# A state-space scan inside a twelve-stage decoder on one Trainium2 core: the scan stage rewritten as 64 unrolled steps, with the convolution folded into the projection and the products with B taken from TensorE

## Chip, cores and metric

One Trainium2 chip, one core. The time is the device time of one execution in microseconds; the kernel before was run three times (median 1649.15, 1648.54 to 1650.21). Everything but the final store lives in the core's on-chip memory. The program is one long sequence of twelve layers ("stages"), each followed by a layer normalisation; the change concerns the fourth of them and the hand-over to it.

## What is computed

The input is x of 4 batches x 256 tokens x 128 features. Stage L1a is a Mamba layer, the reference reads (cut):

```
xn = layer_norm(x) * g + b
u, z = split(xn @ W_in.T)                          # 256 channels each
u = silu(sum_k conv_w[:, k] * pad(u)[k : k+256] + conv_b)   # 4 taps, causal
dt_in, B, C = split(u @ W_x.T)                     # 8, 16 and 16 columns
dt = softplus(dt_in @ W_dt.T + dt_bias)
A = -exp(A_log)
h[t] = exp(dt[t] * A) * h[t-1] + dt[t] * B[t] * u[t]   # for each channel and n < 16
y[t] = sum_n h[t] * C[t]
y = (y + u * D) * silu(z)
out = x + y @ W_out.T
```

After it the decoder adds x once more and normalises the sum, which is the input of the next stage, L1x.

## The kernel before

A feature lies on one of 128 partitions, time runs along the free dimension. The 256 channels make two halves of 128, so a tile for one batch is 128 x 512 (two halves of 256 time steps). All matmuls but those named are float32.

**Class Mamba (L1767 to L2146).** `vector` clears `dA` and `up` (L2013, L2014), takes the statistics of all eight 128-token tiles of X (L2018 to L2024) and writes the eight normalised tiles XN (L2026). TensorE transposes them (L1846), ScalarE copies them out with gain and bias into XNT (L1939). Per batch, `inputs` projects XNT to u and z (L1854, four matmuls of 256 columns), ScalarE copies u out (L1944), VectorE runs the convolution as eight instructions of 256 columns (`convolve`, L2035 and L2037), ScalarE takes silu of both (L1949, L1951). `dt_inputs` and `dts` are the matmuls that give dt_in (L1862), B and C (L1867) and dt's argument (L1873); `arguments` adds the bias (L2045), `logs` on ScalarE computes the parts of softplus (L1959 to L1962), `steps_of_time` on VectorE finishes dt and dt*u (L2065 to L2070) and makes u*D (L2072). `parts` (L2052 to L2059) splits B and C into three bfloat16 parts so that a bfloat16 matmul with a one-hot stationary operand can spread one row of B or C over all partitions (`spread_b` L1890, `spread_c` L1896).

For each batch there are 16 steps, one for each n. A step consists of: `spread_b` on TensorE, its copy to on-chip memory on ScalarE (`b_copy`, L1971), two Exp instructions for dA on ScalarE (`decays`, L1979), the product dB = dt*u*B on GpSimd (L2146, 128x512), the scan along time on VectorE (L2081, with dA and dB both in SBUF), the product with C on VectorE (L2090), and the sum over n on TensorE with the identity (L1884, 512 columns). dA, dB and hC have three buffers, h has two. Three batches run in a hardware loop whose body also prepares the next batch: the convolution is placed between the steps n = 2 to 9, `inputs` at n = 0, silu at n = 11. But `parts`, `steps_of_time` and the last part of `logs` stand behind the last step of a batch, as do the addition of u*D and the gate (L2105, L2106), the output matmuls (L1916) and the two additions that give Z (L2114, L2115).

**Class LayerEnd (L143 to L236)** is the normalisation after each stage: statistics of Z (L177, L180), Ln and Exp on ScalarE for the reciprocal root (L196, L197), three small refinement steps (L138 to L140), eight tiles of X (L188), their transposes (L203) and two copies to XT (L217 or L223, and L227). With `early=True` the first six tiles are handled inside the stage, and only the last two behind it. `keep_warm` (L83) issues bfloat16 matmuls on zeros to a spare bank. The end of L0f, the stage before Mamba, is an early one; that of Mamba is not, and handles all eight tiles after the last batch.

Each engine works through its own instructions in order; the order of the steps is written out by hand, and engines wait for each other through counting semaphores. What an engine must wait for holds up everything behind it in its own order.

## Time and profile before

| | us |
|---|---|
| median of three runs | 1649.15 |
| the profiled execution's own time | 1648.05 |
| its span on the core | 1646.3 |
| last X tile of the end of L0f to the first scan | 528.1 to 561.15 |
| first scan to the start of the 64th | 561.15 to 769.38 |
| start of the 64th scan to the end of the last copy to XT | 769.38 to 784.06 |

Over the whole span TensorE is busy 82%, VectorE 62%, ScalarE 43%, GpSimd 24%. Times in timelines count from the start of the span. A row of a timeline gives start, duration, engine, line, operation, what is written and read, the count of instructions merged in it, and in brackets the idle time before it. One float32 matmul appears as two MATMUL instructions (and two weight loads, PEld); a transpose or a bfloat16 matmul as one. The durations of successive matmuls overlap, so the cost of one in a dense row is the distance of the starts. PEclk is the granted TensorE clock as a share of full speed, 1.00 being 2.4 GHz and 0.50 being 1.2 GHz.

### The profile page before, as it was taken

The page shows a single profiled execution, that of the slowest core. Times are in us where ns is not written, and L with a number is a line of the kernel's source. Part 1 is how long each engine was busy: PE and PEld are TensorE (multiplying, and loading weights), DVE is VectorE, ACT ScalarE, POOL GpSimd, SP SyncE. Part 2 cuts the span into 40 slices and gives each one's busy share as a digit, 9 for nine tenths or more (in the row PEclk, how much of TensorE's full clock was granted, in tenths as well). Part 3 has the DMA queues.
Part 4 walks back from the last instruction along what each step waited for, and adds up shares of the span by engine and source line. Part 5 has one row for each costly group of instructions (what it writes and reads, how often), then busy time and mean ns, then how long its engine had stood idle before and what let it go on. Part 6 is the DMA issues. An engine that isn't in the chain of part 4 may idle for free.

```text
span 1646.3 us, 24843 instructions
## 1 busy us (share of the span) xinstructions
PE 1350.1 (82%) x9010; PEld 839.1 (51%) x9062; DVE 1024.8 (62%) x2330; ACT 700.9 (43%) x1979; POOL 398.6 (24%) x313
## 2 busy tenths in 40 slices
PE   7999766887876567656897647999998999989997
PEld 4665643555554222212554434555566666656664
DVE  2556567666655688888667776755576455643334
ACT  4555324565653545453464303632234555422222
POOL 1333005444420325437400025200100333310000
PEclk9999988999998665678998969999999999999999
DMA  8000000000002200000000000000000000000000
GB/s 355 1 1 1 1 1 1 1 1 2 1 1 89 118 1 0 0 0 0 1 2 0 1 1 1 2 1 1 0 2 2 1 1 1 1 1 0 1 0 13
DMA packets 4217, 24.99 MB, mean 15 GB/s; under 512 B 1168, under 2 KB 3216, under 8 KB 3472
## 3 DMA queue, kind: packets, MB, share of 16 engines
q1 hardware_dynamic: 4112, 23.59, 3.6%
q8 instruction: 66, 1.08, 0.3%
q14 instruction: 39, 0.32, 0.1%
HBM read 23.06 MB, written 0.52 MB: 14 GB/s over the span
## 4 chain that ended last, share of the span: by engine, by line
PE 63%; DVE 20%; issue 8%; ACT 6%; POOL 1%; DMA 1%; DVEq 0%; SPq 0%; POOLq 0%; ACTq 0%
PE PS L1067 5%; PE PS L637 5%; PE PS L1052 4%; PE PS L1053 4%; PE PS L321 4%; PE PS L353 3%; PE PS L333 3%; PE PS L703 3%; DVE arena L2090 2%; PE PS L294 2%; PE PS L302 2%; PE PS L362 2%; PE PS L296 2%; PE PS L315 2%; PE PS L2270 1%
## 5 line engine op out<-in xcount | busy, mean ns | idle before, releaser
L545 POOL TENSOR_TENSOR arena<-arena,small 128x768 f32<-128x768 f32 (+1 forms) x64 | 107.7, 1683 | 225.7 <-DVE small L488 116.7
L873 DVE TENSOR_REDUCE arena<-PS 128x2 f32<-128x512 f32 (+1 forms) x192 | 108.8, 609 | 53.5 <-PE PS L631 52.5
L800 ACT ACTIVATE arena<-PS 128x512 f32<-128x512 f32 (+1 forms) x192 | 92.2, 532 | 107.2 <-PE PS L637 107.2
L1156 DVE TENSOR_TENSOR arena<-arena,PS 128x512 f32<-128x512 f32 x82 | 56.4, 688 | 116.0 <-ACT arena L1089 116.0
L2146 POOL TENSOR_TENSOR arena<-arena 128x512 f32<-128x512 f32 x64 | 103.9, 1643 | 89.5 <-DVE arena L2081 33.0
L1089 ACT ACTIVATE arena<-PS 128x512 f32<-128x512 f32 x82 | 49.0, 597 | 166.0 <-PE PS L1053 166.0
L425 ACT ACTIVATE arena<-PS,small 128x256 f32<-128x256 f32 (+1 forms) x256 | 110.8, 453 | 0.0
L637 PE MATMUL PS<-arena 32*128 32x256 f32 (+1 forms) x768 | 97.5, 370 | 14.0 <-DVE arena L873 8.8
L2081 DVE TENSOR_TENSOR_SCAN arena<-arena 128x512 f32<-128x512 f32 x64 | 94.0, 1473 | 21.7 <-ACT arena L1979 14.3
L1884 PE MATMUL PS<-arena,w_consts 128*128 128x512 f32 x128 | 95.1, 841 | 3.3 <-DVE arena L2090 3.3
L631 PE MATMUL PS<-arena 32*128 32x256 f32 (+1 forms) x768 | 94.5, 371 | 2.2 <-DVE arena L873 1.6
L496 DVE COPY arena<-PS 128x768 f32<-128x768 f32 (+1 forms) x64 | 69.5, 1086 | 34.6 <-PE PS L333 34.5
L637 PEld LDWEIGHTS PS<-arena 32*128 32x128 f32 x768 | 63.8, 185 | 42.8 <-ACT arena L800 31.0
L1067 PEld LDWEIGHTS PS<-w_last,arena 128*128 128x128 f32 x512 | 67.0, 191 | 31.1 <-issue 28.9
L2771 POOL TENSOR_TENSOR arena<-arena 128x512 f32<-128x512 f32 x32 | 40.5, 1267 | 156.2 <-DVE arena L2605 156.2
L1067 PE MATMUL PS<-w_last,arena 128*128 128x128 f32 x512 | 67.7, 275 | 1.0 <-DVE arena L1156 1.0
L1052 PE MATMUL PS<-XT,w_last 128*128 x128 | 66.9, 605 | 0.0
L1053 PE MATMUL PS<-XT,w_last 128*128 x128 | 66.2, 599 | 0.0
L321 PE MATMUL PS<-arena 64*128 64x256 f32 (+1 forms) x512 | 65.9, 376 | 0.0
L2486 ACT ACTIVATE arena<-PS,small 128x128 f32<-128x128 f32 x128 | 45.3, 366 | 46.7 <-DVE small L2633 46.6
L333 PE MATMUL PS<-w_consts,arena 128*128 128x128 f32 x448 | 60.2, 274 | 4.7 <-POOL arena L545 4.6
L631 PEld LDWEIGHTS PS<-arena 32*128 32x128 f32 x768 | 59.6, 185 | 7.1 <-DVE arena L873 4.3
(408 smaller groups left out, 3121.9 us busy)
## 6 DMA issues: line engine op xcount, KB each, us to landing
w_last<-in_last SPq DMA_DIRECT2D x1, 8260.0 KB, 22.6
w_rest<-in_rest SPq DMA_DIRECT2D x1, 5898.5 KB, 36.8
w_last<-in_first SPq DMA_DIRECT2D x1, 4532.5 KB, 21.1
w_last<-in_first SPq DMA_DIRECT2D x1, 2176.0 KB, 10.1
X<-in_x SPq DMA_DIRECT2D x1, 512.0 KB, 4.5
CT<-in_ctxT SPq DMA_DIRECT2D x1, 512.0 KB, 10.8
out<-X SPq DMA_DIRECT2D x1, 512.0 KB, 3.2
w_consts<-in_consts SPq DMA_DIRECT2D x1, 373.0 KB, 3.2
```

The lines of the kernel that those rows point to most:

```text
L321: ins = pe.matmul(PS[:, bank + r, col:col + n], self.QT[rows, p, t * P:(t + 1) * P], self.KT[rows, p, 0:n], start=False, stop=True, skip_g ...
L333: ins = pe.transpose(PS[:, 4 + r, b:b + P], self.Pr[:, i % 3, r, a:a + P], c.ident)
L425: ins = a.activation(self.Pr[:, i % 3, r, col:col + n], PS[:, i % 2 * 2 + r, col:col + n], ACT.Exp, bias=self.nm[:, i % 3, r, t:t + 1], sc ...
L545: g.tensor_tensor(p, p, ri, ALU.mult).then_inc(self.pn_done.sem, 1)
L631: return pe.matmul(PS[:, bank, t * n:(t + 1) * n], self.QP[rows, i % 8, t * P:(t + 1) * P], self.KP[rows, i % 8, t * step:t * step + n], s ...
L637: return pe.matmul(PS[:, 3 + q % 3, t * n:(t + 1) * n], self.KP[rows, i % 8, t * P:(t + 1) * P], self.QP[rows, i % 8, t * step:t * step + ...
L873: v.tensor_reduce(dst, src, AX.X, ALU.max, negate=True).then_inc(self.mx_done.sem, 1)
L1052: pe.matmul(PS[:, j % 2, :], w[:, 0:P], x, start=True, stop=True)
L1053: pe.matmul(PS[:, 2 + j % 2, :], w[:, P:2 * P], x, start=True, stop=True)\
L1067: ins = pe.matmul(PS[:, 4 + e % 2, t * P:(t + 1) * P], self.Hd[0:rows, j % 3, t * P:(t + 1) * P], w, start=(f == 0 and t == 0), stop=(f == ...
L1884: pe.matmul(acc, c.ident, self.hC[:, n % 3, :], start=(n == 0), stop=(n == self.N - 1))\
L2146: g.tensor_tensor(two(self.dB[:, n % 3, :]), self.dtu, b, ALU.mult).then_inc(self.db_ready.sem, 1)
```

## The change

The four batches become one straight sequence of 64 steps g = 16 b + n, without a loop, on every engine.

- The convolution is gone as vector work. A GpSimd instruction of 128 x 1024 multiplies, once, the four taps into copies of the u half of W_in (`WK`); u is then the sum of four matmuls per half over shifted windows of XNT, which has three zero columns ahead of each batch. The convolution's bias goes into the silu instruction.
- B comes with time on partitions (four small matmuls with u stationary, 16 columns). GpSimd builds diagonal matrices from it (`diagonals`, two instructions of 128 x 512 for four steps), dt*u is transposed once per batch (`turn`), and dB is made on TensorE as four matmuls of 128 columns (`drive`) into a bank of PSUM, from which the scan reads it. `b_copy` and the GpSimd product are gone. C is spread with a float32 matmul of 16 rows and 256 columns; `parts` is gone.
- u*D is added on TensorE with diagonal matrices (two matmuls of 256 columns per batch). One vector instruction gives y, one gives Z.
- The bias of dt goes into the two ScalarE passes Abs and Relu; the rest of softplus is five instructions of 128 x 512 on GpSimd (`chain`), for the first batch on VectorE.
- All preparations of batch b+1 are placed among the steps of batch b: on TensorE `inputs` at n = 0, 1, 2, `selections` at 6, `steps` at 8, `turn` at 13; on ScalarE silu at 6, copies at 8, `logs` at 10, the copy of the turned product at n = 1 of the next batch; on VectorE `gate` and `finish` of the batch before at 3 and 5. dA has four buffers.
- The end of Mamba is an early one: six tiles are normalised inside the last batch. The end of L0f makes no XT, since Mamba does not read it, and issues 20 warming matmuls instead. Mamba's own statistics go in groups of two and six tiles.

The diff, cut to its core:

```diff
@@ LayerEnd @@
     def tensor(self, pe):
-        if not self.last:
+        if self.turned:
             keep_warm(self.c, pe, self.spare, 5 if len(self.groups) == 2 else 14)
             self.transposes(pe, len(self.groups) - 1)
             keep_warm(self.c, pe, 3, 4)
+        elif not self.last:
+            keep_warm(self.c, pe, self.spare, 20)
@@ Mamba, tensor @@
+        def inputs(b, part):
...
+            if part < 2:
+                for k in range(4):
+                    ins = pe.matmul(PS[:, self.bank(b, part), part * 256:part * 256 + 256], self.WK[:, k, part * P:(part + 1) * P],
+                                    self.XNT[:, b, k:k + 256], start=(k == 0), stop=(k == 3), skip_group_check=True)
+            else:
...
+                for j in range(2):
+                    ins = pe.matmul(PS[:, 1, j * 256:j * 256 + 256], self.win[:, (2 + j) * P:(3 + j) * P],
+                                    self.XNT[:, b, 3:259], start=True, stop=True, skip_group_check=True)
+            ins.then_inc(self.uz_done.sem, 1)
+        def selections(b):
+            pe.wait_ge(self.us_ready.sem, self.us_ready.at(0, b + 1))
+            u = self.u[:, b % 2, :]
+            for j in range(2):
+                pe.matmul(PS[0:48, 0, 0:256], self.wdc[:, j, :], u[:, j * 256:j * 256 + 256],
+                                start=(j == 0), stop=(j == 1), skip_group_check=True)
+            for t in range(2):
+                for j in range(2):
+                    ins = pe.matmul(PS[:, 0, 256 + t * 16:272 + t * 16], u[:, j * 256 + t * P:j * 256 + t * P + P],
+                                    self.wB[:, j, :], start=(j == 0), stop=(j == 1), skip_group_check=True)
+            ins.then_inc(self.dc_done.sem, 1)
+        def turn(b):
+            pe.wait_ge(self.chain_step.sem, self.chain_step.at(0, 5 * b + 5))
+            pe.wait_ge(self.bt_ev.sem, self.bt_ev.at(0, b + 1))
...
+        def drive(g):
+            b, n = divmod(g, self.N)
+            if n == 0:
+                pe.wait_ge(self.tr_ev.sem, self.tr_ev.at(0, b + 1))
+            if n % 4 == 0:
+                pe.wait_ge(self.diag_ready.sem, self.diag_ready.at(0, g // 4 + 1))
...
+                pe.wait_ge(self.sc_ready.sem, self.sc_ready.at(0, g - 1))
+            for t in range(2):
+                for j in range(2):
+                    ins = pe.matmul(PS[:, 2 + g % 2, j * 256 + t * P:j * 256 + t * P + P],
+                                    self.dtuT[:, b % 2, t, j * P:(j + 1) * P], self.diag[:, g % 12 * 2 + t, :],
+                                    start=True, stop=True, skip_group_check=True)
+            ins.then_inc(self.db_done.sem, 1)
+        def spread(g):
...
+            if g >= 2:
+                pe.wait_ge(self.hc_ready.sem, self.hc_ready.at(0, g - 1))
+            pe.matmul(PS[:, 4 + g % 2, 0:256], self.onehot[32:48, n:n + 1].to_broadcast([16, P]),
+                      self.CB[32:48, b % 2, :], start=True, stop=True).then_inc(self.c_done.sem, 1)
+        def add(g):
...
+            pe.wait_ge(self.hc_ready.sem, self.hc_ready.at(0, g + 1))
+            pe.matmul(PS[:, bank, :], c.ident, self.hC[:, g % 3, :], start=(n == 0), stop=(n == self.N - 1),
+                      skip_group_check=True).then_inc(self.acc_done.sem, 1)
...
+        selections(0)
+        keep_warm(c, pe, 5, 2)
+        steps(0)
+        keep_warm(c, pe, 5, 36)
+        turn(0)
+        drive(0)
+        spread(0)
+        for i in range(self.G):
+            b, n = divmod(i, self.N)
+            if i + 1 < self.G:
+                drive(i + 1)
+                spread(i + 1)
+            if i >= 2:
+                add(i - 2)
+            if b and n == 4:
+                outputs(b - 1)
+            if b + 1 < B:
+                if n < 3:
+                    inputs(b + 1, n)
+                if n == 6:
+                    selections(b + 1)
+                if n == 8:
+                    steps(b + 1)
+                if n == 13:
+                    turn(b + 1)
@@ Mamba, scalar @@
+        def decays(g):
+            b, n = divmod(g, self.N)
+            if n == 0:
+                a.wait_ge(self.chain_step.sem, self.chain_step.at(0, 5 * b + 4))
+            if g >= 4:
+                a.wait_ge(self.sc_ready.sem, self.sc_ready.at(0, g - 3))
...
+                if n == 6:
+                    silus(b + 1)
+                if n == 8:
+                    selections(b + 1)
+                if n == 10:
+                    logs(b + 1)
+            elif n == 10:
+                self.end.root(a, 0)
@@ Mamba, vector @@
+        def scan(g):
+            v.wait_ge(self.da_ready.sem, self.da_ready.at(0, g + 1))
+            v.wait_ge(self.db_done.sem, self.db_done.at(0, g + 1))
+            if g >= 2:
+                v.wait_ge(self.hc_ready.sem, self.hc_ready.at(0, g - 1))
+            v.tensor_tensor_scan(self.h[:, g % 2, :], self.dA[:, g % 4, :], PS[:, 2 + g % 2, :], 0.0,
+                                 ALU.mult, ALU.add).then_inc(self.sc_ready.sem, 1)
...
+        for g in range(self.G):
+            b, n = divmod(g, self.N)
+            scan(g)
+            if g:
+                outputs(g - 1)
+            if b and n == 3:
+                gate(b - 1)
+            if b and n == 5:
+                finish(b - 1)
+            if b == B - 1 and n == 8:
+                self.end.early_stats(v)
+            if b == B - 1 and n == 13:
+                self.end.tiles(v, 0)
@@ Mamba, gpsimd @@
+        g.tensor_tensor(self.WK, self.WK, self.win[:, 0:256].unsqueeze(1).to_broadcast([P, 4, 256]), ALU.mult)\
+            .then_inc(self.wk_ready.sem, 1)
...
+        for b in range(B):
+            for q in range(4):
+                diagonals(4 * b + q)
+            if b + 1 < B:
+                self.chain(g, b + 1)
@@ build @@
-            s.end = LayerEnd(c, s.z_ready, last=i == len(names) - 1, early=isinstance(s, (Attention, NarrowAttention, LocalLayers)),
+            s.end = LayerEnd(c, s.z_ready, last=i == len(names) - 1, early=isinstance(s, (Attention, NarrowAttention, LocalLayers, Mamba)),
```

In `chain` the five instructions are: (ex + 1) - 1, ex - r, + relu, + ln, times u; each waits for the one before. `logs` is two Abs and two Relu of 256 columns, Exp and Ln of 512.

## Rows read from the trace of the kernel before

**Rows 1.** Windows: busy time of each engine, granted clock, DMA, in three stretches of the stage

```profile
core 0: us, PE busy (x) PEld busy (x) DVE busy (x) ACT busy (x) POOL busy (x), PEclk, DMA share, GB/s
528.00:561.15 33.15, 15.17 (x44) 8.51 (x45) 17.55 (x54) 14.41 (x24) 2.64 (x3) 0.65 0.56 239
561.15:769.38 208.23, 135.62 (x326) 48.84 (x325) 180.45 (x206) 103.58 (x228) 105.39 (x66) 0.69 0.00 0
769.38:784.06 14.68, 9.75 (x39) 4.56 (x41) 11.03 (x39) 1.11 (x3) 4.75 (x3) 0.99 0.00 1
```

**Rows 2.** Timeline, steps of the last batch: start, us, engine, line, form

```profile
758.64 1.44 DVE L2081 TENSOR_TENSOR_SCAN arena<-arena 128x512 f32<-128x512 f32 x1
758.96 8.63 POOL L2146 TENSOR_TENSOR arena<-arena 128x512 f32<-128x512 f32 x4
...
760.00 0.66 DVE L2090 TENSOR_TENSOR arena<-arena,PS 128x512 f32<-128x512 f32 x1
...
760.79 1.44 DVE L2081 TENSOR_TENSOR_SCAN arena<-arena 128x512 f32<-128x512 f32 x1
...
769.38 1.23 DVE L2081 TENSOR_TENSOR_SCAN arena<-arena 128x512 f32<-128x512 f32 x1
...
770.52 1.26 DVE L2090 TENSOR_TENSOR arena<-arena,PS 128x512 f32<-128x512 f32 x2
```

**Rows 3.** Timeline, one step of the first batch

```profile
577.61 1.20 DVE L2037 SCALAR_TENSOR_TENSOR arena<-arena,w_rest 128x256 f32<-128x256 f32 x1
...
577.93 1.91 PE L1884 MATMUL PS<-arena,w_consts 128*128 128x512 f32 x2
578.73 1.21 DVE L2081 TENSOR_TENSOR_SCAN arena<-arena 128x512 f32<-128x512 f32 x1
...
579.87 0.66 DVE L2090 TENSOR_TENSOR arena<-arena,PS 128x512 f32<-128x512 f32 x1
```

**Rows 4.** Groups by line and shape, 528 to 561 us

```profile
L2037 DVE SCALAR_TENSOR_TENSOR arena<-arena,w_rest 128x256 f32<-128x256 f32 x6 | 2.9, 485 | 0.2
...
L2026 DVE TENSOR_SCALAR arena<-X,mv,rs 128x128 f32<-128x128 f32 x8 | 2.1, 342 | 0.0
...
L2018 DVE BATCH_NORM_STATS2 bn<-X 128x6 f32<-128x128 f32 x8 | 1.6, 278 | 0.0
...
L2013 DVE MEMSET arena<- 128x1536 f32 x1 | 1.3, 1338 | 0.3 <-issue 0.3
L1949 ACT ACT_TABLE_LOAD x1 | 1.3, 1283 | 0.0
...
L1962 ACT ACTIVATE arena<-arena 128x512 f32<-128x512 f32 x1 | 0.6, 629 | 0.0
```

**Rows 5.** Groups by line and shape, 561 to 777 us: busy, mean ns, idle before

```profile
L2146 POOL TENSOR_TENSOR arena<-arena 128x512 f32<-128x512 f32 x63 | 102.6, 1649 | 76.2 <-DVE arena L2081 33.0 <-ACT arena L1971 23.5 <-DVE arena L2072 19.6
...
L2081 DVE TENSOR_TENSOR_SCAN arena<-arena 128x512 f32<-128x512 f32 x64 | 94.0, 1473 | 21.7 <-ACT arena L1979 14.3 <-DVE arena L2037 2.6 <-DVE arena L2035 1.3
L1979 ACT ACTIVATE arena<-arena 128x255 f32<-128x255 f32 x127 | 56.8, 498 | 4.7 <-DVE arena L2081 4.3
```

**Rows 6.** Windows: a short stretch of the scan stage, and the dense one

```profile
596.00:600.00 4.00, 4.00 (x15) 1.64 (x14) 1.92 (x3) 2.31 (x7) 1.60 (x2) 1.00 0.03 6
1559.00:1570.00 11.00, 11.00 (x51) 6.91 (x50) 4.33 (x9) 2.39 (x4) 0.00 (x0) 1.00 0.00 0
```

**Rows 7.** Timeline, TensorE alone, dense stretches of later stages

```profile
1346.40 1.04 PE L333 MATMUL PS<-w_consts,arena 128*128 128x128 f32 x8
...
1560.63 1.05 PE L1067 MATMUL PS<-w_last,arena 128*128 128x128 f32 x8
1561.53 1.02 PE L1052 MATMUL PS<-XT,w_last 128*128 x2
1562.39 1.02 PE L1053 MATMUL PS<-XT,w_last 128*128 x2
```

**Rows 8.** Timeline, GpSimd, the last instruction before the scan stage's first product

```profile
545.21 1.04 POOL L2138 TENSOR_TENSOR arena<-arena,w_consts 128x512 f32<-128x512 f32 x1 [35.52 <-ACT arena L1951]
```

More of the change, by code:

```diff
@@ L200, in transposes @@
         c = self.c
-        for n in range(*self.groups[g]) if not self.last else ():
+        for n in range(*self.groups[g]) if self.turned else ():
             pe.wait_ge(self.x_tile.sem, self.x_tile.at(0, n + 1))
@@ L214, in vector @@
         self.tiles(v, g)
-        if not self.last and g == 0:
+        if self.turned and g == 0:
             v.wait_ge(self.xt_ps.sem, self.xt_ps.at(0, 1))
@@ L220, in scalar @@
         c, g = self.c, len(self.groups) - 1
-        if g == 1 and not self.last:
+        if g == 1 and self.turned:
             a.wait_ge(self.xt_ps.sem, self.xt_ps.at(0, 1))
@@ new lines, in scalar @@
+        normal(0, 2, 0, 1)
+        silus(0)
+        normal(1, 3, 1, 2)
+        normal(2, 4, 3, 1)
+        selections(0)
+        logs(0)
+        for g in range(self.G):
+            b, n = divmod(g, self.N)
+            if g == 0:
+                decays(0)
+                turned(0)
+            else:
+                decays(g)
+            if n == 1 and b:
+                turned(b)
+            if b + 1 < B:
[7 more added lines that the diff above has]
+                self.end.root(a, 0)
```

543 lines of the change are left out of this document (226 added, 317 removed).

## The prediction

> **What bounds the kernel now.** I read the windows first, to see where the stage begins and ends, then the groups of lines in it, then the timeline of single steps. The scan stage takes 33.15 us to its first scan, 208.23 us from the first to the last scan and 14.68 us to the last copy of XT [rows 1]. In the middle stretch VectorE is busy 180.45 of 208.23 us, TensorE 135.62, ScalarE 103.58 and GpSimd 105.39, and the granted TensorE clock averages 0.69: VectorE is the bound, and TensorE does most of its work at 1.2 GHz, where one sum over n takes 1.91 us [rows 3]. A single step shows what VectorE does. In the last batch, where nothing is prepared, scan follows scan after 760.79 - 758.64 = 2.15 us: 1.36 to the product with C, 0.79 from there to the next scan [rows 2]. With GpSimd idle the first part is 770.52 - 769.38 = 1.14 us [rows 2]. In the first batch a convolution instruction of 1.20 us stands in such a step [rows 3]; the same form took 0.485 us before GpSimd's products began [rows 4]. GpSimd's product takes 1.65 us in the mean and 8.63 / 4 = 2.16 us in the last batch [rows 2, 5]. The two engines hold each other up. The rest of the 208 us is preparation behind each batch's last step.
>
> **The sum: one step.** The change moves 512 columns of products per step to TensorE. Its three parts are priced from a dense stretch at clock 1.00 [rows 6]: four float32 matmuls of 128 columns are 1561.53 - 1560.63 = 0.90 us apart, one of 512 columns 1562.39 - 1561.53 = 0.86 [rows 7]. So `drive` is 0.90, `spread` (256 columns) half of 0.86 = 0.43, `add` 0.86: 2.19 us of TensorE per step. VectorE has 1.14 + 0.79 = 1.93 if the scan runs as it does with GpSimd idle. TensorE becomes the bound. There is a loop through both engines too: `spread`(g+1) waits for the product g-1, and the scan g+1 waits for `drive`(g+1). From a scan's start to the second next it is 1.14 (scan) + 0.66 (product) + 0.43 + 0.86 + 0.90, plus 0.1 each for two hand-overs and 0.15 for the last matmul's end (1.05 - 0.90 [rows 7]) = 4.34, or 2.17 per step. With the scan at 1.36 it is 2.28. The scan now has one operand in SBUF and one in PSUM, a form of which the trace has no row: below it is bounded by 1.14, above by 1.36 with GpSimd running. I take 2.25 for a step: 63 x 2.25 = 141.8 us.
>
> The Trainium skill ("SBUF — State Buffer", Who interferes with whom) says that a VectorE instruction with at most one SBUF input and no two-port mode does not contend with GpSimd. The rows agree as far as they go (two SBUF inputs: 1.36 against 1.14), and by that rule the step would be 2.19 and the total 4 us lower.
>
> **What lies between the steps.** TensorE being the bound, each insertion counts in full. Per prepared batch: `inputs` 10 matmuls of 256 columns at 0.43 = 4.3; `selections` 2 x 0.43 and four tiny ones, which load 128 columns of weights each as `drive` does, 0.9, = 1.8; `steps` 0.86; `turn` four transposes, half of eight at 1.04 [rows 7], = 0.5. That is 7.5 us, three times: 22.4. u*D costs 0.86 four times, 3.4. The output matmuls cost 0.90 three times, 2.7. Together 28.5. The vector instructions `gate` and `finish` (0.66 and less) fit into VectorE's 0.25 us of slack per step, at a stall of a few tenths; the 2.25 holds it. Before, all this (and `parts`) cost at most what 208.23 - 63 x 2.15 = 73 us leaves.
>
> **The new wait.** ScalarE must load another function table for Silu, Exp and Ln, 1.28 us each [rows 4]. Silu at n = 6 is hidden, for the four dA buffers are full then. `logs` at n = 10 starts when `steps` is done, after TensorE's n = 8: four half passes (1.8), Exp 0.63, table 1.28, Ln 0.63, table 1.28, then the pair for dA, 2 x 0.498 [rows 4, 5] = 6.6 us. At that moment the scan 9 is some 2.1 us old, so the scan 11 would be due 3.1 us later. VectorE waits for `decays`(11) about 3.5 us, behind it the product 10, and `spread`(12) on TensorE. Three times: 10.5 us. `chain` on GpSimd begins 2.5 us after `steps` and needs five instructions of 1.04 us alone [rows 8] to 2.16 beside VectorE [rows 2], 6 to 11 us; `turn` at n = 13 comes about 14 us after `steps`, counting the wait, so it is hidden. If the wait of ScalarE were gone, `turn` would be late instead, by up to 3 us. The diagonals (two instructions for four steps, at most 4.3 us of 9) are hidden. The pair for dA (1.0 us of each step) is too. In the last batch the early end puts six statistics (6 x 0.278), a refinement and six tiles (6 x 0.342) on VectorE, 4.3 us of which the slack takes some: 3.5.
>
> Loop: 141.8 + 28.5 + 10.5 + 3.5 = 184.3 against 208.2: -24 us.
>
> **Before the first scan.** Off the path go a memset (1.34), eight convolution instructions (8 x 0.485 = 3.9), six of the eight normalised tiles ahead of the first projection (1.6) [rows 4], and one pass each on VectorE and ScalarE less four half passes for one, 0.6. On it come six more matmuls of 256 columns (2.6) and the turned product in place of GpSimd's (0.8). The granted clock was 0.65 there [rows 1]; with 20 and 36 warming matmuls I expect the high level for most of it, worth 3. Sum -7; at the low level 0, and all of it at its best -10. GpSimd's product of the taps runs in the 35.52 us in which it idled [rows 8] and costs nothing.
>
> **Behind the last scan.** Six of eight statistics and tiles (0.75 x (2.2 + 2.7), by [rows 4]'s means 278 and 342) are -3.7, of which about 1 was overlapped; six transposes -0.8 [rows 7]; two vector instructions less, of 0.66 and 0.4, -1.1. Sum -5.
>
> **Total:** -24 - 7 - 5 = -36. The profiled execution took 1648.05, so 1612; the median of the runs stands 1.1 higher: 1613 us.
>
> **Rivals.** *TensorE keeps the low level (slower).* The place is the loop. Its 63 x 2.19 + 28.5 = 166.5 us of TensorE work hold at clock 1.00; at a granted mean c they are 166.5 / c. At the old 0.69 that is 241, with some 7 us of the waits left 248: +40, less 9 at the ends, so 1680 us. The point from which it decides: 166.5 / c + 14 = 208.2 + 9, c = 0.82. For it speaks that TensorE stayed at 0.69 while busy 65% of the time [rows 1]; against it, that it is at 1.00 where it was busy throughout, even for 4 us inside this stage [rows 6], and that it now never waits long but for three stops of 3.5 us. 6%.
>
> The Trainium skill ("TensorE: Matmul & The Clock Gate", HAM oscillation) says that pauses between bursts of matmuls bring the half rate back. By it each of the three stops would be followed by some steps at 1.2 GHz, 5 us or so apiece by the rows' prices, and the total near 1628, inside the range.
>
> *The hand-overs cost more.* A step with waits on three semaphores on TensorE costs 2.45, as when each group's first matmul starts cold; 63 x 0.2 = 12.6, and `chain` at 2.16 per instruction makes `turn` late by 3 us three times: 1613 + 22 = 1635. For it speaks that GpSimd's products did take 2.16 beside the scan. 16%.
>
> *ScalarE's wait is absorbed.* If `logs` starts earlier or Abs, Relu and Exp need no new table, and the step is 2.19, 10.5 + 4 go: 1599. 14%.
>
> *The scan from PSUM is slow, or the change fails of its purpose.* A scan 0.35 us longer makes VectorE's 2.28 the bound, near 1617, within the forecast. That the work moved to TensorE just eats the gain, at a mean clock near 0.82, is 1649: 2%.
>
> The forecast has 62%. A measurement of this kernel can tell some 0.2%, 3.3 us, from no change. The range holds the absorbed wait and the dear hand-overs: 1595 to 1636. Faster 0.93, same 0.02, slower 0.05.
>
> **What would show it.** Right: granted clock above 0.9 between the first and last scan; TensorE busy above 90%; scans 2.2 to 2.3 us apart in plain steps; a wait of VectorE for ScalarE's Exp near each batch's step 11; scans of 1.2 us, whether GpSimd runs or not; first scan at 554, last at 738. Wrong: scans over 2.4 us apart in plain steps; TensorE waiting for GpSimd (`turn`, diagonals) for more than 2 us a batch; a clock of 0.7.

## The result, and the profile after

The changed kernel takes 1627.45 us (median of 4 runs, 1626.36 to 1628.41) against 1648.85 for the kernel before (1647.86 to 1650.21): ratio 0.9871, 95% interval 0.9858 to 0.9884. It is 21.4 us faster where 36 were forecast. The profiled execution took 1626.36, its span is 1624.5.

The windows of the three stretches of the stage, as in [rows 1] (columns as there: stretch, length, busy time and instructions of PE, PEld, DVE, ACT, POOL, then the granted clock, DMA share and GB/s):

```profile
528.00:553.96 25.96, 22.53 (x106) 13.36 (x105) 9.63 (x40) 15.57 (x29) 6.21 (x6) 0.93 0.71 306
553.96:754.18 200.22, 193.25 (x911) 127.72 (x911) 119.34 (x153) 85.52 (x174) 47.28 (x41) 0.98 0.00 1
754.18:766.58 12.40, 8.21 (x35) 4.30 (x35) 8.21 (x19) 2.98 (x5) 4.75 (x3) 1.00 0.00 0
```

The prologue went from 33.15 to 25.96 us, the loop from 208.2 to 200.2, the stretch behind the last scan from 14.7 to 12.4. TensorE is now busy 193.25 of 200.22 us at clock 0.98, and VectorE 119 instead of 180. These three differences make 17.5 us of the 21.8 between the spans. The other 4.3 us lie behind the stage, in code that is the same in both kernels: from the last copy of XT to the end it took 862.24 us before and 857.92 after, and in the kernels below 859 to 866. TensorE was busy 759.0 us of it before and 753.6 after, VectorE 501.2 and 501.9. The change did not aim at these 4.3 us and the forecast has no term for them. So lengths inside the stage are compared below as well as totals.

The groups of lines in the loop, by form (busy, mean ns | idle before, and what ended it), to be held against [rows 5]:

```profile
L2104 DVE TENSOR_TENSOR_SCAN arena<-arena,PS 128x512 f32<-128x512 f32 x64 | 78.1, 1220 | 81.3 <-PE PS L1890 70.3 <-ACT arena L2021 10.3
...
L1890 PEld LDWEIGHTS PS<-arena 128*128 128x128 f32 x504 | 66.8, 196 | 21.8 <-issue 21.3
...
L2157 POOL TENSOR_TENSOR arena<-w_consts,arena 128x512 f32<-128x512 f32 x26 | 26.4, 1042 | 57.5 <-PE PS L1890 57.5
...
L1912 PEld LDWEIGHTS PS<-arena,w_consts 128*128 128x128 f32 x120 | 18.0, 190 | 20.2 <-issue 20.2
```

The scan (L2104) waits 70.3 us for `drive` (L1890) and 10.3 us for ScalarE's exponentials (L2021). The scan with one operand in PSUM takes 1.22 us whether GpSimd runs or not, and GpSimd's remaining product (the diagonals, L2157) 1.04 where its old one took 1.65. And the weight loads of `drive` and of `add` (L1912) each stand idle some 21 us for "issue", which nothing recorded explains. That is the first sign of what went wrong in the forecast.

The timeline of plain steps, on VectorE, TensorE and TensorE's weight loads (start, us, engine, line, form, idle before):

```profile
571.98 1.22 DVE L2104 TENSOR_TENSOR_SCAN arena<-arena,PS 128x512 f32<-128x512 f32 x1 [0.77 <-PE PS L1890]
...
574.55 1.22 DVE L2104 TENSOR_TENSOR_SCAN arena<-arena,PS 128x512 f32<-128x512 f32 x1 [0.77 <-PE PS L1890]
...
570.83 1.05 PE L1890 MATMUL PS<-arena 128*128 128x128 f32 x8
571.81 0.69 PE L1903 MATMUL PS<-arena,w_consts 16*128 16x256 f32 x2
572.44 1.12 PE L1912 MATMUL PS<-arena,w_consts 128*128 128x512 f32 x2
573.40 1.05 PE L1890 MATMUL PS<-arena 128*128 128x128 f32 x8
...
571.81 0.29 PEld L1903 LDWEIGHTS PS<-arena,w_consts 16*128 16x128 f32 x2
572.43 0.30 PEld L1912 LDWEIGHTS PS<-arena,w_consts 128*128 128x128 f32 x2 [0.33 <-issue]
```

A plain step is 574.55 - 571.98 = 2.57 us. From start to start `drive` (L1890) takes 0.98, `spread` (L1903) 0.63, `add` (L1912) 0.96, where the forecast had 0.90, 0.43 and 0.86. TensorE waits for no other engine here. VectorE waits 0.77 us for `drive` in each step, so TensorE sets the pace. The last two rows show that the load of `spread` starts with its own matmul, at 571.81, and that of `add` at 572.43, with the matmul at 572.44: neither runs ahead under the matmul before it.

### The profile page after: what moved, and what is told of

Its sections match the earlier page's. It is cut to its first block, busy times and chain, and to the rows that moved or that the text cites. A ratio compares the mean times of both kernels' runs of the same rounds, so it can differ in the third digit from the quotient of the medians.

```text
span 1624.5 us, 25636 instructions
## 1 busy us (share of the span) xinstructions
PE 1413.6 (87%) x9708; PEld 918.2 (57%) x9708; DVE 953.5 (59%) x2240; ACT 685.6 (42%) x1932; POOL 348.1 (21%) x293
## 4 chain that ended last, share of the span: by engine, by line
PE 72%; DVE 15%; ACT 6%; issue 4%; POOL 1%; DMA 1%; DVEq 0%; SPq 0%; ACTq 0%; POOLq 0%
PE PS L1071 6%; PE PS L641 5%; PE PS L1056 4%; PE PS L1057 4%; PE PS L325 4%; PE PS L1912 4%; PE PS L357 3%; PE PS L1890 3%; PE PS L337 3%; PE PS L707 3%; PE PS L1903 2%; PE PS L298 2%; PE PS L306 2%; PE PS L366 2%; PE PS L319 2%
## 5 line engine op out<-in xcount | busy, mean ns | idle before, releaser
L2104 DVE TENSOR_TENSOR_SCAN arena<-arena,PS 128x512 f32<-128x512 f32 x64 | 78.1, 1220 | 81.3 <-PE PS L1890 70.3
L641 PE MATMUL PS<-arena 32*128 32x256 f32 (+1 forms) x768 | 97.7, 371 | 13.8 <-DVE arena L877 9.5
L641 PEld LDWEIGHTS PS<-arena 32*128 32x128 f32 x768 | 64.0, 185 | 42.3 <-ACT arena L804 30.4
L1071 PEld LDWEIGHTS PS<-w_last,arena 128*128 128x128 f32 x512 | 66.9, 191 | 32.7 <-issue 28.7
L1890 PEld LDWEIGHTS PS<-arena 128*128 128x128 f32 x512 | 67.7, 196 | 22.7 <-issue 21.3
L2792 POOL TENSOR_TENSOR arena<-arena 128x512 f32<-128x512 f32 x32 | 40.6, 1269 | 156.0 <-DVE arena L2626 156.0
L2021 ACT ACTIVATE arena<-arena,w_rest 128x255 f32<-128x255 f32 x128 | 55.5, 497 | 41.7 <-DVE arena L2104 40.7
L1912 PE MATMUL PS<-arena,w_consts 128*128 128x512 f32 x128 | 72.5, 652 | 0.0
L1890 PE MATMUL PS<-arena 128*128 128x128 f32 x512 | 69.8, 280 | 0.7 <-ACT arena L2011 0.7
## 6 DMA issues: line engine op xcount, KB each, us to landing
w_last<-in_first SPq DMA_DIRECT2D x1, 4532.5 KB, 21.4
w_last<-in_first SPq DMA_DIRECT2D x1, 2176.0 KB, 10.3
```

Of the source, the lines that this page charges most:

```text
L641: return pe.matmul(PS[:, 3 + q % 3, t * n:(t + 1) * n], self.KP[rows, i % 8, t * P:(t + 1) * P], self.QP[rows, i % 8, t * step:t * step + ...
L1071: ins = pe.matmul(PS[:, 4 + e % 2, t * P:(t + 1) * P], self.Hd[0:rows, j % 3, t * P:(t + 1) * P], w, start=(f == 0 and t == 0), stop=(f == ...
L1890: ins = pe.matmul(PS[:, 2 + g % 2, j * 256 + t * P:j * 256 + t * P + P], self.dtuT[:, b % 2, t, j * P:(j + 1) * P], self.diag[:, g % 12 * ...
L1912: pe.matmul(PS[:, bank, :], c.ident, self.hC[:, g % 3, :], start=(n == 0), stop=(n == self.N - 1), skip_group_check=True).then_inc(self.ac ...
```

## Experiments

Below, "loop" is the length from the first to the last scan and "tail" that from the last scan to the last copy of XT; the changed kernel, called after, has 200.2 and 12.4 us. Each ratio is to the kernel before as it ran beside the kernel in question (medians 1648.0 to 1650.1), so totals of two kernels that differ by 2 us or less are not told apart.

### 1. ScalarE's logarithms two steps later

The question: what does the stop of VectorE for ScalarE cost in the end, and is it VectorE's wait or `turn` that decides?

```diff
-                if n == 10:
+                if n == 12:
                     logs(b + 1)
```

> `logs` moved on ScalarE from n = 10 to n = 12, so the pairs for scans 11 and 12 are made before it. Theory S (the three stops at step 11 cost what the trace of the changed kernel shows net: 585.60 to 590.83 is 5.23 instead of 2.57, of which the next scan wins back 0.64, so 2.0 to 2.2 each): 6.0 to 6.6 us less, 1621. Rival (the stop is cover for GpSimd's chain, and turn is late instead): 0 to 3 us less, with TensorE waiting before the transposes of dt*u.

1624.12 us (1622.64 to 1625.58), ratio 0.9851 (0.9828 to 0.9873). The stops are gone, plain steps stay at 2.57, `turn` isn't late, and the loop is 190.6 us, 9.6 shorter, more than the 6.0 to 6.6 expected. The total shows only 3.3 of that, half of what was expected of it, since in this profile the code before the first scan took 4.3 us longer and that behind the stage 4.5 (862.5 us). In after's timeline of VectorE the three stops can be read one by one. The first and the second:

```profile
585.60 1.22 DVE L2104 TENSOR_TENSOR_SCAN arena<-arena,PS 128x512 f32<-128x512 f32 x1 [2.02 <-PE PS L1890]
...
590.83 1.22 DVE L2104 TENSOR_TENSOR_SCAN arena<-arena,PS 128x512 f32<-128x512 f32 x1 [3.43 <-ACT arena L2021]
...
595.42 1.22 DVE L2104 TENSOR_TENSOR_SCAN arena<-arena,PS 128x512 f32<-128x512 f32 x1 [0.86 <-PE PS L1890]
...
643.91 1.22 DVE L2104 TENSOR_TENSOR_SCAN arena<-arena,PS 128x512 f32<-128x512 f32 x1 [3.43 <-ACT arena L2021]
...
654.30 1.22 DVE L2104 TENSOR_TENSOR_SCAN arena<-arena,PS 128x512 f32<-128x512 f32 x1 [2.92 <-PE PS L1890]
```

VectorE waits 3.43 us, close to the 3.5 forecast. But TensorE worked ahead meanwhile, so after the first stop a short step of 1.93 us follows (the next scan starts at 592.76): 595.42 - 585.60 = 9.82 us for three steps that otherwise take 7.71, a net cost of 2.1. The third stop costs 2.1 as well. The second began at 638.68 and needed 15.62 us for four steps that take 10.28, a net 5.3, since TensorE ran at its lower level for a while (experiment 10). 2.1 + 5.3 + 2.1 = 9.5, within 0.1 of the 9.6 that this kernel saves. The expectation had priced all three stops as the first.

### 2. A wait that is already met, inside `drive`

Is the dear step a price of waits, which TensorE's first instruction after a wait pays?

```diff
             for t in range(2):
+                if t:
+                    pe.wait_ge(self.wk_ready.sem, self.wk_ready.at(0, 1))
                 for j in range(2):
```

> One more wait per step on TensorE, on a semaphore that was reached long before, between the second and the third matmul of drive. Theory W (each wait keeps the weight load behind it from running ahead, so that it stands in the open at about 0.10 us): steps 2.67 instead of 2.57 us apart, 6 us more in all, 1634. Theory L (the 0.38 us above the sum of the matmuls comes from the loop through VectorE, scan to product to spread): no change, 1627, because TensorE would have that slack.

1634.35 us in two runs, ratio 0.9916 (0.9887 to 0.9945). Plain steps remain at 2.57 (scans at 569.02, 571.59, 574.16, 576.73), so a met wait costs nothing that one step shows. The total is 6.9 higher, of which the loop has 1.6 (201.8 us) and the rest lies outside it. The total alone would have misled.

The loop's 1.6 us come from the granted clock. In after it fell behind the second of ScalarE's three stops alone; here it fell behind each:

```profile
593.00:603.00 10.00, 8.14 (x28) 5.09 (x29) 6.62 (x8) 4.97 (x12) 7.04 (x7) 0.83 0.00 0
647.00:657.00 10.00, 7.97 (x32) 5.08 (x30) 5.93 (x7) 5.66 (x14) 7.72 (x7) 0.83 0.00 1
702.00:712.00 10.00, 7.97 (x29) 4.99 (x29) 6.24 (x7) 5.35 (x13) 7.39 (x7) 0.83 0.00 0
```

From the scan ahead of a stop, the five steps take 15.86 us in kernel 1, which has no stop; 17.97, 21.20 and 17.96 in after; and 19.58, 19.57 and 19.58 here. So the three stops cost 11.1 us net here and 9.5 in after.

### 3. `add` ahead of `spread`

Is it `add`, after the small matmul, that is dear, or whatever stands beside it?

```diff
                 drive(i + 1)
-                spread(i + 1)
             if i >= 2:
                 add(i - 2)
+            if i + 1 < self.G:
+                spread(i + 1)
```

> On TensorE the sum over n now stands before spread instead of behind it (drive, add, spread); spread's wait for VectorE's product is then met 0.9 us earlier. Theory W: 2.57 us per step as before, within 0.05. Theory L: the loop loses 0.86 us over two steps, so the step falls to 2.2 to 2.3 and the total by 17 us or more.

1624.69 us in two runs, ratio 0.9857 (0.9829 to 0.9886); plain steps 2.57 again. So neither theory holds: W (the price of a wait) wanted 2.67 in experiment 2, L (the loop through VectorE) wanted 2.2 to 2.3 here. The timeline of TensorE's weight loads:

```profile
571.15 0.30 PEld L1912 LDWEIGHTS PS<-arena,w_consts 128*128 128x128 f32 x2
572.22 0.29 PEld L1903 LDWEIGHTS PS<-arena,w_consts 16*128 16x128 f32 x2 [0.76 <-issue]
572.84 0.97 PEld L1890 LDWEIGHTS PS<-arena 128*128 128x128 f32 x8 [0.33 <-DVE arena L2105]
```

Now `add`'s load runs ahead of its matmul (571.15, the matmul starts at 571.26), and those of `spread` and of `drive` behind it don't (572.22 and 572.84, with their matmuls). In either order it is the load of the 16-row matmul and the one that follows it. The loop still fell to 191.1. TensorE now waits only 1.17 us at each stop instead of 2.04, as `add` is done ahead of the wait. The first stop's steps were 5.23, 1.93, 1.93 and 2.44, a net 1.25 instead of 2.1, and the clock did not fall after any stop. That accounts for 2.6 and 3.2 of the 9.1 us. Of the rest, 2.4 are the step behind `steps` (3.01 for 3.83, three times) and 0.6 that behind `selections` (4.46 for 4.65).

### 4. `add` in pairs

Two sums one behind the other share their hand-over. This takes a fourth hC buffer and its waits (cut here).

```diff
-            if i >= 2:
+            if i >= 3 and i % 2:
+                add(i - 3)
                 add(i - 2)
```

> The sums over n of two steps are issued together every second step, with one wait for both, and hC has four buffers; columns and matmuls stay. Theory W: one wait and one exposed weight load fewer in two steps, 0.05 us per step, 3 us less, 1624. Theory L: no change or worse, since the products of two steps are awaited together.

1640.34 us (1639.6 to 1643.62), ratio 0.9954 (0.9938 to 0.997), the loop 203.5, 3.3 longer; of the total's 12.9 us, 8.1 lie behind the stage. A miss: the steps alternate between 1.93 and 3.5 us (scans at 571.55, 573.48, 577.00), and in the short one TensorE waits for the product again ("[0.23 <-DVE arena L2114]"). That two buffers of dB and of C are too few for work in bunches is the likely reason; no run here varies them.

### 5. `spread` over all 128 rows

If it is the 16-row operand, the same broadcast with a one-hot column of 128 rows must remove the cost. CB is zeroed once, so that its unused rows add nothing to the sum.

```diff
-            pe.matmul(PS[:, 4 + g % 2, 0:256], self.onehot[32:48, n:n + 1].to_broadcast([16, P]),
-                      self.CB[32:48, b % 2, :], start=True, stop=True).then_inc(self.c_done.sem, 1)
+            pe.matmul(PS[:, 4 + g % 2, 0:256], c.ident[:, 32 + n:33 + n].to_broadcast([P, P]),
+                      self.CB[:, b % 2, :], start=True, stop=True).then_inc(self.c_done.sem, 1)
...
+        v.memset(self.CB, 0.0).then_inc(self.cb_clear.sem, 1)
```

> `spread` takes a one-hot column of the identity as a stationary operand of 128 rows (instead of 16 rows at partition 32) and all 128 rows of CB, of which the unused ones are zero; columns and waits stay. Theory R (the 0.38 us per step above the sum of the matmuls stands before and behind the 16-row matmul, because weight loads do not run ahead across it): the weight loads of spread and of add start before the matmul ahead of them has ended, the steps fall from 2.57 to 2.19 to 2.3 us, the loop by 15 to 22 us and the total to 1606 to 1613. Theory I (the cost is one of issuing the instructions of TensorE, or of its waits): nothing changes, 2.57 us and 1627.

1610.26 us (1609.2 to 1611.55), ratio 0.976 (0.9744 to 0.9776): 17 us faster than after by one edited matmul and the memset that it needs. The loop is 181.4, 18.9 shorter. Its timeline of steps:

```profile
570.13 1.22 DVE L2107 TENSOR_TENSOR_SCAN arena<-arena,PS 128x512 f32<-128x512 f32 x1 [0.41 <-PE PS L1891]
...
572.31 1.22 DVE L2107 TENSOR_TENSOR_SCAN arena<-arena,PS 128x512 f32<-128x512 f32 x1 [0.38 <-PE PS L1891]
...
568.98 1.05 PE L1891 MATMUL PS<-arena 128*128 128x128 f32 x8
569.87 0.60 PE L1904 MATMUL PS<-arena,w_consts 128*128 128x256 f32 x2
570.31 1.02 PE L1913 MATMUL PS<-arena,w_consts 128*128 128x512 f32 x2
571.17 1.05 PE L1891 MATMUL PS<-arena 128*128 128x128 f32 x8
...
569.77 0.30 PEld L1904 LDWEIGHTS PS<-arena,w_consts 128*128 128x128 f32 x2
570.09 0.41 PEld L1913 LDWEIGHTS PS<-arena,w_consts 128*128 128x128 f32 x2
```

A step is 2.18 us, and `drive`, `spread`, `add` are 0.89, 0.44 and 0.86 apart, the forecast's terms to a hundredth. The loads start 0.10 and 0.22 us before their matmuls.

The Trainium skill ("TensorE: Matmul & The Clock Gate", Step-by-step: what each phase is for) says that the queue pulls a weight load ahead of a running matmul when their row groups don't conflict or the load goes to the background buffer, and that the number of rows of the weights doesn't matter for its time. The trace agrees on the load's own time: 0.29 us for `spread` with 16 rows and 0.30 with 128. What the rows change is when it starts: with 16 it isn't pulled ahead, nor is the next, and the step takes 2.57 us instead of 2.18.

The trace of the kernel before held this already, in other stages. A load of 128 rows behind a 128-row matmul (L611 behind L615), then one behind 32-row matmuls (L631):

```profile
785.82 0.76 PEld L611 LDWEIGHTS PS<-CT,w_rest 128*128 128x128 f32 x2
786.25 1.02 PE L611 MATMUL PS<-CT,w_rest 128*128 128x256 f32 x2
...
787.68 1.15 PE L631 MATMUL PS<-arena 32*128 32x256 f32 x16
788.75 0.30 PEld L611 LDWEIGHTS PS<-CT,w_rest 128*128 128x128 f32 x2 [0.33 <-issue]
788.76 1.12 PE L611 MATMUL PS<-CT,w_rest 128*128 128x512 f32 x2
```

The first runs 0.43 us ahead, the second 0.01. It is so throughout that trace: of the float32 loads of 128 rows and columns for a matmul that follows another without a gap, none of the 56 behind 32-row weights and none of the 63 behind 64-row weights runs ahead, and none of the 58 behind weights of 128 rows but 64 columns; but all 59 behind the 96-row bfloat16 weights of the old `spread_b` and `spread_c` do, by 0.11 us or more. Where neighbours of 32 rows follow each other, loads do run ahead, by up to 0.39 us. So the rows fit a cost of the change between a short and a full operand, not of shortness alone.

### 6 and 7. The full-height `spread` with the later logarithms, and with the order of 3 as well

> The full-row spread together with logs at n = 12. If both act for themselves: the loop 9 to 10 us below that of the full-row spread alone, total 1597 to 1604. Rival (with faster steps GpSimd's chain of 7.2 us is late, and TensorE waits before the transposes of dt*u): less than half of the 9 us is kept.

> As the run before, and the sum over n ahead of spread. With the stops gone the order should bring little: 0 to 3 us less. If it brings over 3 us, the order helps in plain steps too, by giving VectorE's product more time.

The first: 1601.26 us (1599.64 to 1602.27), ratio 0.9703 (0.9687 to 0.972), loop 168.9. The second: 1597.8 (1597.34 to 1598.17), ratio 0.9683 (0.9667 to 0.9699), loop 167.3. Taken one after the other, the loop fell by 18.9 us for the rows, 12.4 for the stops and 1.6 for the order. With the shorter step the stops were dearer than in experiment 1 (9.6): against kernel 6 they cost experiment 5 a net 4.7, 3.0 and 4.7, and the clock fell after the first and the third, to 0.85 and 0.90 in stretches of 10 us. In kernel 7 TensorE was busy 166.5 of 167.3 us at clock 1.00, so little but its own work is left in this loop.

### 8. A scan with both operands in SBUF

The scan reads dA for both operands; the products dB are still made but not used. This tells whether the steady 1.22 us comes from the operand in PSUM or from GpSimd's lighter load.

```diff
-            v.tensor_tensor_scan(self.h[:, g % 2, :], self.dA[:, g % 4, :], PS[:, 2 + g % 2, :], 0.0,
+            v.tensor_tensor_scan(self.h[:, g % 2, :], self.dA[:, g % 4, :], self.dA[:, g % 4, :], 0.0,
```

> The scan takes dA as both operands, so it reads two tensors from on-chip memory and none from PSUM; dB is still made but not read (the result leaves dB out). Theory P (two operands in SBUF make the scan and GpSimd hold each other up): scans of 1.4 us and more where GpSimd runs, GpSimd's instructions of 1.04 us stretched to 1.3 to 2.2, first-to-last scan 0 to 5 us longer because TensorE has the bound. Rival (the 1.22 us is due to something else): scans of 1.22 us throughout.

1633.15 us in one run, loop 204.4. Its timeline, a stretch where GpSimd works:

```profile
595.49 1.04 POOL L2157 TENSOR_TENSOR arena<-w_consts,arena 128x512 f32<-128x512 f32 x1
...
595.68 1.93 DVE L2104 TENSOR_TENSOR_SCAN arena<-arena 128x512 f32<-128x512 f32 x1 [0.64 <-PE PS L1890]
...
598.32 1.23 DVE L2104 TENSOR_TENSOR_SCAN arena<-arena 128x512 f32<-128x512 f32 x1
...
598.41 1.97 POOL L2157 TENSOR_TENSOR arena<-w_consts,arena 128x512 f32<-128x512 f32 x1
```

Both scans stand beside a product of GpSimd, and of each two the one that starts first keeps its length. The product of 595.49 took its usual 1.04 us, and the scan that began 0.19 behind it 1.93. The scan of 598.32 took 1.23, and the product that began 0.09 behind it 1.97. The products' mean rises from 1.04 to 1.46 us, the longest scan is 2.11. With one operand in PSUM (after) no scan takes over 1.22 us and the products' mean stays at 1.04. The Trainium skill's rule ("SBUF — State Buffer", Who interferes with whom), of which [rows 2] showed only the half with two inputs, holds here in both halves.

### 9. The next stage's memset in four parts

After's tail is 2.7 us longer than forecast. Its timeline shows two normalised tiles at 2.70 us beside a memset of the next stage:

```profile
762.81 2.70 DVE L190 TENSOR_SCALAR X<-Z,mv,rs 128x128 f32<-128x128 f32 x2
...
761.86 3.51 POOL L971 MEMSET arena<- 128x4096 f32 x1
```

The pair ends at 765.51 and the memset at 765.37. The same memset stood in the kernel before:

```profile
777.85 3.51 POOL L967 MEMSET arena<- 128x4096 f32 x1
...
780.38 2.66 DVE L188 TENSOR_SCALAR X<-Z,mv,rs 128x128 f32<-128x128 f32 x8
```

There the tiles began 0.98 us before it ended; the early end brings the last two to where 2.56 us of it are left. On top of kernel 7:

```diff
-        g.memset(self.V, 0.0).then_inc(self.cleared.sem, 1)
+        for n in range(0, 8, 2):
+            ins = g.memset(self.V[:, n:n + 2, :], 0.0)
+        ins.then_inc(self.cleared.sem, 1)
```

> The fastest kernel so far (spread over 128 rows, logarithms at step 12, add ahead of the spread) with the next stage's memset of V on GpSimd issued in four parts of 128x1024. Theory M (the memset of 3.51 us held the last two X tiles: 2.70 us for the pair in after, where the tiles before took 0.60 for two): the stretch from the last scan to the last XT copy falls from 12.4 us by 1 to 2, the two last tiles take 0.6 to 1.3 us together, and the kernel is 1595.8 to 1596.8, 1 to 2 us below the same without the split. Rival (the tiles wait for something else, or the four parts hold them just as long, one after the other): the stretch keeps its length within 0.3 us and the kernel stays at 1597.3 to 1598.2.

1597.35 us (1596.86 to 1598.56), ratio 0.9693 (0.9677 to 0.9709). The same two groups, in this kernel:

```profile
729.83 1.04 DVE L190 TENSOR_SCALAR X<-Z,mv,rs 128x128 f32<-128x128 f32 x2
...
728.88 3.77 POOL L972 MEMSET arena<- 128x1024 f32 x4
```

The pair takes 1.04 us and the tail 10.32 instead of 12.01: 1.7 gained there, as expected. The medians differ by 0.45 us, within their own spread: the gain is shown in the stage, not in the total. In the two profiles the code behind the stage took 3.0 us longer here (863.6 against 860.6) and that ahead of the first scan 1.8 less.

### 10. No warming matmuls

The 20 + 4 + 2 + 2 + 36 matmuls that only keep TensorE busy ahead of the first scan are left out of after.

```diff
-            keep_warm(self.c, pe, self.spare, 20)
+            pass
...
-            keep_warm(c, pe, 5, warm)
...
-        keep_warm(c, pe, 5, 2)
         steps(0)
-        keep_warm(c, pe, 5, 36)
```

> After without the matmuls that only keep TensorE busy ahead of the first scan. If they earn their place (the clock of the prologue, 0.93 in after, falls to 0.5 to 0.8 and its matmuls double), the stretch from the stage's first instruction to the first scan grows from 26.0 us to 29 to 32 and the total by 3 to 6 us, to 1630 to 1634; the loop keeps its 200.2 within 1.5, its clock at 0.95 or more from the second batch on. If the clock is held by the projections anyway, the stretch stays within 1 us of 26.0 and the total within 1.5 us of 1627.5.

1648.69 us (8 runs, 1646.89 to 1653.22), ratio 1.0009 (0.9999 to 1.002): the whole gain of the change is gone. Both cases expected were wrong. From the last X tile to the first scan it takes 28.2 us (clock 0.62) instead of 25.9, only 2.3 more, but the loop grew by 17.2, to 217.4. Of these, 4.3 are its first two steps, before any stop, and 12.9 lie at the three stops. The windows behind the stops:

```profile
600.00:610.00 10.00, 9.36 (x23) 5.78 (x24) 4.18 (x6) 3.75 (x9) 5.96 (x6) 0.53 0.01 2
660.00:670.00 10.00, 10.00 (x26) 5.94 (x26) 3.90 (x5) 1.76 (x4) 4.01 (x5) 0.55 0.01 2
...
720.00:730.00 10.00, 10.00 (x27) 6.08 (x27) 3.60 (x4) 0.91 (x2) 1.93 (x2) 0.50 0.01 2
```

After each of ScalarE's three stops TensorE ran 10 to 14 us at 1.2 GHz. After has the same stops, with the same wait of TensorE, and its clock fell after the second alone. Its windows there:

```profile
640.00:650.00 10.00, 7.96 (x34) 5.39 (x33) 4.49 (x6) 7.93 (x15) 9.49 (x8) 0.86 0.00 1
650.00:660.00 10.00, 10.00 (x41) 6.36 (x40) 5.10 (x7) 3.20 (x7) 3.26 (x4) 0.80 0.00 0
```

And the timeline of TensorE at a stop, first after, then the kernel of this experiment, in a fence each:

```profile
645.76 0.69 PE L1903 MATMUL PS<-arena,w_consts 16*128 16x256 f32 x2 [2.04 <-DVE arena L2112]
...
647.58 1.92 PE L1890 MATMUL PS<-arena 128*128 128x128 f32 x8
```

```profile
600.64 1.22 PE L1902 MATMUL PS<-arena,w_consts 16*128 16x256 f32 x2 [2.04 <-DVE arena L2109]
...
603.65 1.92 PE L1889 MATMUL PS<-arena 128*128 128x128 f32 x8
```

The wait is 2.04 us in both. In after the matmul behind it still runs at the full rate (0.69) and `drive` at half (1.92 for 1.05); here already the first is slow (1.22). Without the warming, the first stop and its half rate cost 610.52 - 593.55 = 16.97 us for four steps of 2.57, a net 6.7 against 2.1 where the clock held.

The warming alone doesn't decide whether the clock falls. Of the kernels that keep it, with the same wait of 2.03 to 2.04 us at each stop, it fell after one stop in after and in experiment 11, after two in experiment 12, and after all three in experiments 2 and 4, in 10 of 15 cases. Experiment 2 changes nothing ahead of the first scan. In experiment 3, where TensorE waits 1.17 us, it fell after none. Nor does the warming bound how low it goes: in experiment 8 it was 0.50 from 647 to 657 us. Shown is that without the warming the gain is lost, in all 8 runs; whether the missing matmuls themselves did it, or the later and slower start of the loop that came with it, is open, since no run has one without the other. By the five steps of experiment 2, a stop cost 2.1 us net where the clock held and 3.7 to 8.6 where it fell (22.81, 22.80 and 24.43 us here). In kernels 1, 6, 7 and 9 there is none, and the clock is 1.00 throughout.

### 11. The stage's end late, as before

```diff
-            s.end = LayerEnd(c, s.z_ready, last=i == len(names) - 1, early=isinstance(s, (Attention, NarrowAttention, LocalLayers, Mamba)),
+            s.end = LayerEnd(c, s.z_ready, last=i == len(names) - 1, early=isinstance(s, (Attention, NarrowAttention, LocalLayers)),
```

The calls that went with it (statistics at n = 8, tiles at n = 13, the first transposes) are taken out too.

> After with the stage's end as it was in before: statistics, X tiles and their transposes all behind the last scan. The early end costs the loop nothing where VectorE has slack, so if it is worth what its hidden work is (two sets of tiles and transposes of four channel groups each, 2.14 us a set in before, less the copies that TensorE's loop makes wait), the stretch from the last scan to the last XT copy grows from 12.4 to 14 to 15.5 us and the total by 1.5 to 3 us, to 1629 to 1630.5, the loop staying within 1 us of 200.2. If the insertions cost TensorE's loop as much as they save, the loop falls by 1 to 2 us and the total stays within 1 us of 1627.5.

The two runs lie at 1630.5 and 1639.2 us (ratio 0.9919, 0.9888 to 0.995), too far apart to compare with after by the total. In the profile of the first the tail is 13.8 instead of 12.4 and the loop 199.3 instead of 200.2. That is just below the 14 to 15.5 expected, with the loop as expected. So in after the early end earns 1.4 us behind the last scan and costs 0.9 in the loop, a net 0.5. With the memset out of its way (experiment 9) its tail is 1.7 shorter still.

### 12. `spread` over 48 rows

Which matters, that the operand starts at row 32 or that it is short? The edit is shown against kernel 5:

```diff
-            pe.matmul(PS[:, 4 + g % 2, 0:256], c.ident[:, 32 + n:33 + n].to_broadcast([P, P]),
-                      self.CB[:, b % 2, :], start=True, stop=True).then_inc(self.c_done.sem, 1)
+            pe.matmul(PS[:, 4 + g % 2, 0:256], c.ident[0:48, 32 + n:33 + n].to_broadcast([48, P]),
+                      self.CB[0:48, b % 2, :], start=True, stop=True).then_inc(self.c_done.sem, 1)
```

> Spread with a one-hot of 48 rows from row 0 (after: 16 rows from row 32, plain step 2.57; the 128-row form: 2.18 to 2.21). If only a full-height operand keeps the weight loads hidden, a plain step is 2.55 to 2.60 and the kernel 1623 to 1628. If what hurts is that the operand starts at row 32 and not that it is short, a plain step is 2.18 to 2.25, and the kernel 1608 to 1613.

1631.27 us in two runs, ratio 0.9898 (0.9878 to 0.9917); loop 200.3, as in after. The weight loads:

```profile
571.49 0.29 PEld L1904 LDWEIGHTS PS<-arena,w_consts 48*128 48x128 f32 x2
572.12 0.30 PEld L1913 LDWEIGHTS PS<-arena,w_consts 128*128 128x128 f32 x2 [0.33 <-issue]
```

Their durations and the idle time between them are after's, and the step is 2.57, as the first case expected of the step. It is the height, not the start row: 16 and 48 rows cost 0.39 us a step more than 128. No run has a float32 `spread` of a height between 48 and 128. The total is 3.8 above after's, outside the 1623 to 1628 expected, with the same loop and tail, which again is the code outside the stage (862.7 us behind it, against 857.9).

## Why the prediction was right or wrong

**Right in its main mechanism, short by one term, and helped by luck.** The time fell in the range, and TensorE became the bound at a high clock: 0.98 in the loop against "above 0.9", busy 97% against "above 90%", a scan of 1.22 us against 1.2, the first scan at 553.96 against 554, GpSimd never waited for by TensorE. The slower rival, TensorE at the low level throughout, is refuted by the clock of 0.98. Two of the signs named for being right did not come: scans 2.2 to 2.3 us apart and the last one at 738 (it started at 754.18). One of those named for being wrong did: scans over 2.4 us apart in plain steps. Inside the stage 36 us were forecast and 17.5 came, less than half; the other 4.3 us between the spans are code that the change doesn't touch, and no credit to the forecast.

**The step that failed is "I take 2.25 for a step".** It measured 2.57, so 63 x 0.32 = 20.2 us were missing. The sum of three prices from dense rows [rows 7] was right in itself: with a full-height `spread` the step is 2.18. But [rows 7] shows 128-row matmuls following one another, and `spread` was priced as half of one, by its columns alone. It has 16 rows, and the load of a short operand and the one after it don't run ahead of the matmul before. The rows of L611 in experiment 5 show that the trace of before had this to read. The rival "hand-overs cost more" had 2.45, a size near the truth with the wrong cause: a further met wait costs a step nothing (experiment 2), the order neither (3), the rows all of it (5, 12).

**The loop's account.** Forecast 184.3, measured 200.2. The steps give +20.2. The three stops cost 9.5 instead of 10.5: VectorE's wait was 3.43 as forecast (3.5), but two of them cost 2.1 net, since TensorE had worked ahead, and one 5.3. Insertions and the last batch's early end were put at 22.4 + 3.4 + 2.7 + 3.5 = 32.0; without stops the loop is 190.6, of which 63 x 2.57 = 161.9 are steps and 28.7 are left, so -3.3. Most of that is the early end, put at 3.5 and worth 0.9 by experiment 11. Together +20.2 - 1.0 - 3.3 = +15.9.

**The clock.** The forecast's sentence on pauses, that each stop would be followed by steps at 1.2 GHz with the total near 1628, met the total by chance: in after one stop of three was, and most of the missing time lies in the plain steps. In experiments 2 and 4 all three are, and without the warming matmuls too. The Trainium skill's rule ("TensorE: Matmul & The Clock Gate", HAM oscillation) is borne out as a possibility of each pause, not as its certain result. The 3 us that the forecast gave the warming for the prologue were 2.3; that leaving it out would lengthen the loop by 17.2 us was not foreseen at all.

**Before the first scan** -7 was forecast and -7.2 measured, though the parts were not measured apart from the warming.

**Behind the last scan** -5 was forecast and -2.3 measured. Of the missing 2.7, 1.7 are the next stage's memset, which held two tiles (experiment 9). [rows 4] priced those tiles at 342 ns with nothing beside them; here 2.70 us for two. Another 0.4 is rounding, since the forecast's own terms, -3.7 + 1 - 0.8 - 1.1, make -4.6 and not -5. The last 0.6 was not taken apart.

**`turn` late** was part of the rival with 1635. It was not late in any kernel here: GpSimd's chain took 1.27 us in four of its instructions and 1.93 in the first, and even with the logarithms two steps later it was done in time.

**A slip in a rival.** A scan 0.35 us longer would make VectorE's step 2.28, 0.03 above the 2.25 taken, so 1615 and not 1617. Nothing rests on it.

## What to carry to other kernels

Where TensorE is the bound, price a matmul by its rows as well as its columns: a stationary operand of 16 or 48 rows between full ones cost 0.39 us each time, and padding it to 128 rows with zeros gave back 17 us for no more work per column. Look in the trace at hand for a load of the same shape between the same neighbours before taking its price from another shape. A stop that another engine absorbs in length can still cost TensorE its clock, so remove stops before counting on the high level; the best kernels here (full-height `spread`, later logarithms, `add` first, with the memset split or not) take 1597.35 and 1597.8 us, 0.9693 and 0.9683 of the kernel before, with TensorE busy 166.5 of 167.3 us in the loop. And compare stretches of the profile when totals differ by a few us: code that no edit touched moved by up to 8 us between these kernels.

## What was not expected of the hardware

- A float32 matmul of 16 or 48 rows between full ones keeps its own weight load and the next one from running ahead: 2.57 us a step against 2.18 at 128 rows.
- The same wait of TensorE, 2.04 us three times in the loop, left the clock high or brought it down, from kernel to kernel: after one stop in the changed kernel, after all three with one more met wait in each `drive` (0.83 in stretches of 10 us), and after all three without the warming matmuls (0.53, 0.55 and 0.50).
- A memset on GpSimd, which reads nothing, held VectorE's normalised tiles: 2.70 us for two beside one of 3.51 us, 1.04 beside four quarters of it.
- A scan with two SBUF operands and a GpSimd product stretched whichever of them started second: the scan from 1.23 to up to 2.11 us, the product from 1.04 to 1.97. With one operand in PSUM the scan stayed at 1.22.
